# Layer-norm steps of the next tile placed sooner in the q/k/v stage of a macaron block

## What is computed

```
q = silu(short_conv_1d(x @ Wq + bq, q_conv))      # k, v the same, x is layernorm(x)
q = q / (norm(q over a head) + 1e-6)              # k the same
alpha, beta = sigmoid(x @ Wa + ba), sigmoid(x @ Wb + bb)
out_gate = silu(x @ Wg + bg)
layernorm(x) = (x - mean(x)) / sqrt(var(x) + 1e-5)
```

## Time and profile before

| | |
|---|---|
| median of 3 runs | 3521.77 us (3519.32 to 3527.73) |
| profiled execution, its own time | 3522.09 us |
| its span | 3520.3 us |
| TensorE busy in the span | 3247.0 us (92%) |
| VectorE busy | 2775.2 us (79%) |
| ScalarE busy | 1567.9 us (45%) |
| GpSimd busy | 1832.7 us (52%) |

### The profile page before, as it was taken

One profiled execution on the slowest core, in us unless ns is written; L12 is line 12 of the kernel. 1 busy time (PEld: TensorE's weight loads), 2 busy tenths in 40 slices (PEclk: granted clock), 3 DMA queues, 4 the chain that ended last, 5 costly groups with the idle time before them and its releaser, 6 DMA issues. The chain is left out here.

```text
span 3520.3 us, 192119 instructions
## 1 busy us (share of the span) xinstructions
PE 3247.0 (92%) x83236; PEld 2732.5 (78%) x83236; DVE 2775.2 (79%) x4456; ACT 1567.9 (45%) x2328; POOL 1832.7 (52%) x1707
## 2 busy tenths in 40 slices
PE   7999998698989999894999999999996987999999
PEld 5888886476666667673999999999995765888887
DVE  6767765788888888874899999999997866676765
ACT  4555453577777777772121211121213433545454
POOL 1232322466666666654778888778884431222232
PEclk8999999799999999997999999999997998999999
DMA  3122222232323223224677777777774772212121
GB/s 120 71 101 78 91 88 86 84 91 90 92 86 98 88 79 107 74 86 126 185 201 202 198 200 201 199 199 198 201 199 138 235 226 111 100 71 107 71 107 60
DMA packets 486556, 452.96 MB, mean 129 GB/s; under 512 B 55504, under 2 KB 448848, under 8 KB 467280
## 3 DMA queue, kind: packets, MB, share of 16 engines
q1 hardware_dynamic: 484176, 449.56, 42.4%
q10 hardware_dynamic: 2304, 2.49, 0.3%
HBM read 331.33 MB, written 120.60 MB: 128 GB/s over the span
## 5 line engine op out<-in xcount | busy, mean ns | idle before, releaser
L350 POOL TENSOR_TENSOR ffn_out<-ffn_gate,ffn_xres 128x512 f32<-128x512 f32 x128 | 179.9, 1437 | 781.5 <-DVE ffn_gate L254 781.1
L803 DVE SCALAR_TENSOR_TENSOR ain_conv<-ain_padded,ain_taps,ain_conv 128x512 f32<-128x512 f32 x384 | 447.7, 1166 | 13.6
L1480 ACT ACTIVATE rec_u<-rec_ps_end 128x256 f32<-128x256 f32 x128 | 49.0, 383 | 632.4 <-PE rec_ps_end L1532 632.4
L902 POOL TENSOR_TENSOR ain_conv<-ain_conv,ain_term 128x512 f32<-128x512 f32 x192 | 281.3, 1465 | 16.0
L1248 POOL TENSOR_TENSOR rec_d_norm<-rec_dmat,rec_early 128x512 f32<-128x512 f32 x128 | 162.7, 1271 | 174.7 <-DVE rec_dmat L1330 174.7
L957 ACT ACTIVATE ain_buf<-ain_conv 128x512 f32<-128x512 f32 x192 | 120.9, 630 | 244.5 <-POOL ain_conv L902 158.8
L46 PE MATMUL ffn_ring<-ffn_mixkh,ffn_wkh 128*128 128x512 f32 x512 | 218.8, 427 | 6.5 <-DVE ffn_mixkl L196 6.5
L46 PE MATMUL ffn_ring<-ffn_mixrh,ffn_wrh 128*128 128x512 f32 x512 | 215.6, 421 | 9.2 <-DVE ffn_mixrl L306 9.2
L899 POOL TENSOR_SCALAR ain_term<-ain_padded,ain_taps 128x512 f32<-128x512 f32 x192 | 185.9, 968 | 39.7 <-POOL ain_conv L902 26.4
L46 PE MATMUL ffn_ring<-ffn_mixkh,ffn_wkl 128*128 128x512 f32 x512 | 203.3, 397 | 0.0
L46 PE MATMUL ffn_ring<-ffn_mixrh,ffn_wrl 128*128 128x512 f32 x512 | 202.3, 395 | 0.0
(11 more groups left out here) (252 smaller groups left out, 10218.7 us busy)
## 6 DMA issues: line engine op xcount, KB each, us to landing
rec_early<-coeffs SPq DMA_DIRECT2D x512, 128.0 KB, 3.0
streams<-ain_buf SPq DMA_DIRECT2D x48, 1024.0 KB, 5.1
rec_qkv<-streams SPq DMA_DIRECT2D x126, 384.0 KB, 3.3
rec_qk_pe<-streams SPq DMA_DIRECT2D x127, 256.0 KB, 3.3
rec_late<-coeffs SPq DMA_DIRECT2D x504, 64.0 KB, 2.3
ffn_xres<-in_x SPq DMA_DIRECT2D x16, 1024.0 KB
ain_x<-x SPq DMA_DIRECT2D x16, 1024.0 KB, 4.8
gate<-ain_gate SPq DMA_DIRECT2D x16, 1024.0 KB, 6.6
```

The source lines that it names most:

```text
L350: added = nc.gpsimd.tensor_tensor(out[:, m, :], gate[:, m, :], xres[:, m, :], ALU.add)
L803: nc.vector.scalar_tensor_tensor(out=out[:], in0=pad[:, n:n + TOK], scalar=taps[:, u // KT, u % KT, n:n + 1], in1=out[:], op0=ALU.mult, op ...
L902: nc.gpsimd.tensor_tensor(out[:], out[:], term[:], ALU.add).then_inc(pool_conv, 1)
L1480: nc.scalar.activation(u[:], ps_end[:, :, 1, :], ACT.Copy).then_inc(u_ready, 1)
```

## The change

It moves five steps of the chain of tile t + 1. `deviations` is split: the new function `variances` (adding epsilon) stands on VectorE behind convolution 4, ahead of `decays`; what is left of `deviations` (reciprocal and diagonal) stands ahead of convolution 6 where it stood behind it. `normalise` stands ahead of convolution 7 where it stood behind it. On ScalarE the root stands behind Silu 4 (it stood behind Silu 5) and `high` behind Silu 7 (it stood behind Silu 8). On TensorE the spread stands behind group 10 (it stood behind group 11). No instruction is added or taken away.

```diff
--- before.py
+++ after.py
@@ -765,9 +765,11 @@
                 nc.vector.tensor_tensor(xc[:], x[:], ps_mean[:].unsqueeze(1).to_broadcast([P, KT, TOK]),
                                         ALU.subtract).then_inc(centred, 1)
 
-            def deviations(t):
+            def variances(t):
                 dve.wait_ge(var_done, t + 1)
                 nc.vector.tensor_scalar_add(var_tok[:], ps_mean[:, 0:KT], LN_EPS).then_inc(var_copied, 1)
+
+            def deviations(t):
                 dve.wait_ge(std_ready, t + 1)
                 nc.vector.reciprocal(rstd_tok[:], std_tok[:]).then_inc(inverted, 1)
                 dve.wait_ge(inverted, t + 1)
@@ -829,15 +831,17 @@
                     centre(t + 1)
                 for u in (0, 1, 3, 4):
                     convolve(t, u)
+                if ahead:
+                    variances(t + 1)
                 decays(t)
                 if ahead == 2:
                     sums(t + 2)
+                if ahead:
+                    deviations(t + 1)
                 convolve(t, 6)
                 if ahead:
-                    deviations(t + 1)
+                    normalise(t + 1)
                 convolve(t, 7)
-                if ahead:
-                    normalise(t + 1)
                 convolve(t, 9)
                 if ahead:
                     low(t + 1, 1 - s)
@@ -851,6 +855,7 @@
             weight_high("k")
             select_heads()
             dve.wait_ge(ident_step, 2)
+            variances(0)
             deviations(0)
             weight_low("k")
             normalise(0)
@@ -976,9 +981,9 @@
                         act.wait_ge(ab_done, t + 1)
                         act.wait_ge(coeff_stored, COEFF_DMAS * t)
                         nc.scalar.activation(alpha_beta[:], ps_ab[:], ACT.Sigmoid, bias=ab_bias[:]).then_inc(ab_ready, 1)
-                    if more and u == 7:
+                    if more and u == 6:
                         deviation(t + 1)
-                    if more and u == 10:
+                    if more and u == 9:
                         high(t + 1, 1 - s)
                 act.wait_ge(heads_summed, HEADS_0 + 2 * t + 2)
                 nc.scalar.activation(inv_norm[:], ps_rows[:], ACT.Sqrt).then_inc(rooted, 1)
@@ -1061,7 +1066,7 @@
                         head_sums(t, u // 4 - 2)
                     if more and u == 7:
                         var(t + 1)
-                    if more and u == 11:
+                    if more and u == 10:
                         spread_rstd(t + 1)
 
             pe.wait_ge(ready, 1)
```

## The result

The changed kernel took 3536.3 us (median of 5 runs, 3530.5 to 3539.4) against 3519.3 us for the kernel before on the same chip: a ratio of 1.004, 95% interval 1.002 to 1.006. It is slower, by 17 us. The profiled execution took 3530.5 us, with a span of 3528.7; it is the fastest of the five, 8.4 us above the profiled one of the kernel before.

A forecast was written before the change was run, and what follows sets the result against it. Bound: a ring of GpSimd's convolutions and ScalarE's shifts and Silus in the q/k/v stage. Root 1.41, rounding 1.81 and overlap 0.1 gave 3.33 us a slot, 50 us over 15 slots: 3522.1 to 3472 us, range 3458 to 3504.

The forecast's parts named there:

- The ring of GpSimd and ScalarE: In the q/k/v stage, GpSimd's convolutions and ScalarE's shifts and Silus release each other; shortening it gains 3.33 us a slot.
- the root's part: On ScalarE, table load and root leave the path to shift 8 and move behind Silu 4: 1.41 us a slot.
- the rounding's: On ScalarE, the rounding leaves its place between Silu 8 and shift 11, moving ahead of shift 10: 1.81 us a slot.
- I take the sum of both as unchanged: On VectorE, convolutions 6 and 7 together keep their old time, 5.3 + 2.6 us, so convolution 7 ends at 1056.5.
- no reserve: Convolution 11 could start at 1063.1 or 1063.2 by two paths; each microsecond convolution 7 ends after 1056.6 is lost.
- named as a rival: Late convolution 7 on VectorE: it takes 5.3 us too, leaving 0.6 us a slot, 3513 us; chance 0.10.
- Against it: the new waits are shorter and head sums lie between them: The reason given against a clock fall on TensorE, where groups 13 to 14 wait for square 7 and shift 10.
- The clock rival: TensorE's clock halves in groups 14, 15 and ab, costing 1.4 or 3.05 us a slot: 3493 or 3518 us; chance 0.10.
- The slower rival: Convolutions 6 and 7 meet GpSimd in every multiply-add, 6.2 us each: 1.2 us a slot lost, 3540 us; chance 0.04.
- the two milder rivals: Late convolution 7 (3513 us, chance 0.10) and TensorE's clock falling at a worse place (3493 or 3518 us, chance 0.10).
- the three signs of being wrong: Silu 8 well behind convolution 8's end; clock 0.50 in groups 14, 15 or ab; VectorE busy over a microsecond more per slot.
- a root's part of 2.8 us: By the Trainium skill's 2.66 us per table switch on ScalarE, the root's part would be 2.8 us, the time about 3453.

The follow-up runs named there:

- e1: Changed kernel with normalisation back behind convolution 7 and rounding back behind Silu 8, so only the root's part remains: 3503.3 us, ratio 0.994.
- e2: Kernel before with only the rounding moved ahead of shift 10: 3493.2 us, ratio 0.992.
- e5: Changed kernel with normalisation put back behind convolution 7: 3460.5 us, ratio 0.983.
- e3: Changed kernel with 8 extra matmuls ahead of the second head sums and 8 behind them, filling TensorE's two waits: 3494.8 us, ratio 0.991.
- e6: Kernel of e5 with 8 extra matmuls behind the second head sums: 3454.3 us, ratio 0.981.
- e8: Changed kernel with the rounding put back behind Silu 8, normalisation still ahead of convolution 7: 3487.9 us, ratio 0.991.
- e9: Changed kernel with 8 extra matmuls only ahead of the second head sums, the wait behind them left open: 3499.8 us, ratio 0.995.
- e4: Kernel before with 16 extra matmuls ahead of the spread, filling TensorE's wait there: 3529.8 us, ratio 1.002.

## Why the prediction was wrong

Forecast was 3472 us and faster; it came out at 3536 and slower.

- **The ring of GpSimd and ScalarE as the bound, and its two terms: right.** Alone, the root's part gives 1.9 us where the clock does not fall (e1; 1.41 and 0.1 were reckoned) and the rounding's 1.8 (e2; 1.81). Together, with convolution 7 on time, the slot is 56.63 us (e5), 0.6 below the 57.2 forecast, by what GpSimd's own convolutions got shorter.
- **"I take the sum of both as unchanged": the step that failed first.** Convolutions 6 and 7 were put at 5.3 + 2.6 = 7.9 us. The prediction read the 2.33 us of convolution 7 as those of a convolution beside an idle GpSimd. GpSimd was not idle: in the earlier trace rows its copies for convolution 8 start at 1053.38, in the middle; what convolution 7 did not meet were GpSimd's additions. In the changed kernel convolution 6 took from the diagonal's end at 1050.86 to 1054.91, 4.1 us, and convolution 7 from the normalisation's end at 1057.10 to 1061.96, 4.9 us, together 8.9; reciprocal and diagonal took 1.53 us (1049.33 to 1050.86), where 0.96 was reckoned. Convolution 6 got better and 7 got worse, as said, but not by equal parts. That made convolution 7 end 1.6 us late, 1.0 by the two convolutions and 0.6 by the diagonal. With "no reserve", as the text itself had it, the ring lost 1.25 us of its 3.33 (convolution 11 starts at 1068.26, less 3.91 1064.35, against 1066.42). This was named as a rival and given one chance in ten; with the clock held, normalisation's place costs 2.2 us a slot (e3 against e6), or 33 us.
- **"Against it: the new waits are shorter and head sums lie between them": the step that failed second.** The clock rival was right in its mechanism, and nearly in its place (group 14 and the start of group 15 ran slow; the coefficient product was only late). The reason against it was wrong. Behind two waits of about 2 us with 1.06 us of head sums between them the clock fell in every slot, for 6.8 us in 14 of 15. It costs 2.4 us a slot (e3), 35 us; 1.4 to 3.05 were named.
- **The rivals were priced one by one, and they are not independent.** The late convolution 7 opens both waits through Silu 7's square and through shift 10; the rounding ahead of shift 10 makes the second one longer. Take away either the early normalisation (e5) or the early rounding (e8), and the clock does not fall or its fall is free. The prediction's own prices, 1.0 us for a convolution 7 that is a microsecond late and 3.05 for the long fall, come with its 57.25 to 61.3 us a slot; 61.25 was measured. So close a match is partly luck, since the terms measured are 56.63, 2.2 and 2.4. But adding the two rivals would have given the sign.
- **The slower rival** (every multiply-add of both convolutions at its longest) did not happen, and that its 3540 us lie near the measured 3536 is luck: VectorE's busy time rose by 0.4 us a slot (766.0 to 772.1 us in 15). The slowdown came from the two milder rivals in one. Of the three signs of being wrong that the prediction named, two were there: Silu 8 started 2.35 us behind the end of GpSimd's convolution 8, and the clock was 0.50 in group 14.
- **A slip that changed nothing:** a root's part of 2.8 us is 1.39 us more than 1.41, so the time for it would have been 3451 us, not 3453. In the changed kernel too the root starts 0.01 us behind its table load (1047.80 + 1.28, then 1049.09).
- **The Trainium skill's rule on the ports to SBUF that VectorE and GpSimd share** (SBUF — State Buffer, SBUF: two separate sides) was the warning that should have had more weight. By it whichever of the two starts first keeps them for its whole instruction. The trace agrees: in the changed kernel the copy that took 1.15 us ends at 1058.37, 0.03 us behind an addition of GpSimd that ran from 1057.05 to 1058.34, and the multiply-adds beside GpSimd's next instructions took 3.56 us; in e5 the same copy, with GpSimd idle, took 0.17 us and the multiply-adds 2.33.

What decides in which repetition of a slot the clock falls stays open; only the price of a fall at each place is measured.

## What to carry to other kernels

When several steps of a chain are moved at once, look at each for what it gets in front of: normalisation went ahead of a convolution on which Silu, rounding, a shift and TensorE's next group were waiting, and one step put back turned a loss of 17 us into a gain of 58. A wait that is taken from TensorE at a place with slack (here at the spread, where the fall of the clock was free in the kernel before) and comes back ahead of work that the next tile waits for costs its own length and, where the clock falls behind it, more, so price lateness and clock together. Slack is used up by gains, too: with the slot 1.8 us shorter (e2) the long fall at the same spread cost 1.2 us. Extra matmuls into a free bank are a cheap way to ask what the clock costs: they made the changed kernel faster by 41 us and left the kernel before as it was.

## What the runs showed that was not expected

- A wait of 3.05 us ahead of group 15 was followed by a fall of the clock in 10 slots of e1 and by none in 5; one of 1.98 us by a fall in 6 slots of e9 and by none in 9; one of 2.15 us by a fall in 11 slots of e4. In each of these kernels the wait was of that length in all 15 slots, within 0.2 us. A single wait's length does not decide it; the same slot, repeated, comes out either way. There is an order in it: in the kernel before the long fall came in slots 1, 4, 7, 10 and 13, every third. No run here shows what makes it.
- A fall in the slots lasted 3.4 or 6.8 us, and its price went with its length and its place: 0.8 and 2.0 us in e1, about 1.5 us for a short one in e9 and 1.0 in e4, nothing for a short one and 1.2 us for a long one in e2, nothing in the kernel before and in e8.
- Filling one wait of TensorE can move the fall to the next one, where it costs: e4 removed the free fall at the spread and got one in group 15, 6 us slower in all.
